# The skip term D u written into the sum's PSUM bank by ScalarE, TensorE's state sums added onto it

## The reference, cut to what matters

```python
delta = softplus(dt @ W_dt.T + b_dt)          # 1024 inner channels, 128 positions
def step(h, ins):                             # 16 states for each inner channel
    d_t, B_t, C_t, u_t = ins
    dA = exp(d_t[..., None] * A)
    h = dA * h + (d_t * u_t)[..., None] * B_t[:, None, :]
    y_t = einsum('bds,bs->bd', h, C_t)        # sum over the 16 states
    return (h, y_t)
y = scan(step) + u * Dp                       # the skip term D u
y = y * silu(z)                               # the gate
return y @ W_out.T
```

## Time and profile before

| | |
|---|---|
| median of 3 runs | 4119.69 us (4118.02 to 4127.19) |
| the profiled execution | 4124.45 us |
| its span, first to last instruction | 4122.3 us |
| mean granted TensorE clock | 0.95 of full speed |
| busy: TensorE, VectorE, ScalarE, GpSimd | 87%, 88%, 70%, 84% of the span |

### The profile page before, as it was taken

One profiled execution on the slowest core, in us unless ns is written; L12 is line 12 of the kernel. 1 busy time (PEld: TensorE's weight loads), 2 busy tenths in 40 slices (PEclk: granted clock), 3 DMA queues, 4 the chain that ended last, 5 costly groups with the idle time before them and its releaser, 6 DMA issues. The chain is left out here.

```text
span 4122.3 us, 44370 instructions
## 1 busy us (share of the span) xinstructions
PE 3597.6 (87%) x11386; PEld 2046.1 (50%) x11386; DVE 3607.9 (88%) x3165; ACT 2868.8 (70%) x6098; POOL 3455.2 (84%) x1860
## 2 busy tenths in 40 slices
PE   6888888988888988888988888988888988888887
PEld 3644554545554545554544554554554554554443
DVE  0499988999989999889998989999999899989898
ACT  1577667777667777667777667777767777767775
POOL 0298888898888998888998888898888898888899
PEclk8899999999999999999999999999999999999999
DMA  2111101111101111101111101111101111101110
GB/s 100 49 51 53 53 9 47 50 53 53 53 8 48 50 53 53 53 8 48 50 53 53 53 8 48 50 53 53 53 9 47 50 53 53 53 8 44 47 47 8
DMA packets 50702, 183.68 MB, mean 45 GB/s; under 512 B 7339, under 2 KB 33203, under 8 KB 42067
## 3 DMA queue, kind: packets, MB, share of 16 engines
q1 hardware_dynamic: 48880, 174.17, 11.0%
q10 hardware_dynamic: 1636, 7.83, 0.5%
HBM read 164.15 MB, written 17.83 MB: 44 GB/s over the span
## 5 line engine op out<-in xcount | busy, mean ns | idle before, releaser
L411 POOL TENSOR_TENSOR st<-st,bc 128x1024 f32<-128x1024 f32 x1024 | 2399.4, 2358 | 474.2 <-DVE st L870 473.0
L870 DVE TENSOR_TENSOR_SCAN st<-dec,st 128x1024 f32<-128x1024 f32 x1024 | 2311.9, 2277 | 78.0 <-ACT dec L464 63.6
L464 ACT ACTIVATE dec<-delta,decay 128x254 f32<-128x254 f32 x4096 | 1695.1, 465 | 713.4 <-DVE st L870 712.4
L685 PE MATMUL y_ps<-st,ident 128*128 128x512 f32 x4096 | 1975.9, 611 | 184.2 <-POOL st L411 182.8
L685 PEld LDWEIGHTS y_ps<-st,ident 128*128 128x128 f32 x4096 | 756.5, 194 | 999.8 <-issue 599.7
L858 DVE TENSOR_TENSOR st<-du,bc 128x1024 f32<-128x1024 f32 x736 | 885.5, 1203 | 34.3 <-ACT du L450 34.3
L402 POOL TENSOR_TENSOR st<-du_sb,bc 128x1024 f32<-128x1024 f32 x288 | 679.3, 2359 | 0.1
L896 DVE SCALAR_TENSOR_TENSOR u<-d_ps,chan,u 128x250 f32<-128x250 f32 (+2 forms) x768 | 309.4, 473 | 160.9 <-ACT u L504 159.2
L705 PE MATMUL g<-wo,zs 128*128 128x256 f32 x1024 | 300.2, 446 | 0.8 <-DVE zs L877 0.8
L705 PEld LDWEIGHTS g<-wo,zs 128*128 128x128 f32 x1024 | 230.8, 229 | 128.8 <-issue 92.1
L681 PE MATMUL y_ps<-u,diag 128*128 128x256 f32 x512 | 168.5, 459 | 127.7 <-DVE zs L877 127.6
(11 more groups left out here) (106 smaller groups left out, 2775.1 us busy)
## 6 DMA issues: line engine op xcount, KB each, us to landing
bc<-bc_dram SPq DMA_DIRECT2D x64, 2048.0 KB, 9.8
xg<-x_dram SPq DMA_DIRECT2D x32, 256.0 KB, 11.5
x_dram<-xg SPq DMA_DIRECT2D x32, 256.0 KB, 2.0
last_x<-x_dram SPq DMA_DIRECT2D x32, 256.0 KB, 2.6
out_dram<-last_x SPq DMA_DIRECT2D x32, 256.0 KB, 2.1
bc<-w_inT_dram ACTq DMA_DIRECT2D x1, 4096.0 KB
adjt<-adjT_dram SPq DMA_DIRECT2D x32, 128.0 KB, 11.2
bc<-w_out_dram ACTq DMA_DIRECT2D x1, 2048.0 KB
```

Source lines behind the costliest of these rows:

```text
L411: nc.gpsimd.tensor_tensor(st[:, sl, :, :, :], st[:, sl, :, :, :], bc[:, p, 1, SU * q:SU * q + SU, None, :].to_broadcast([P, SU, 2, T]), AL ...
L464: a = nc.scalar.activation(dec[:, v % 2, s, j, :].rearrange("p (b t) -> p b t", b=PAIR)[:, :, 1:], delta[:, p, 2 * i + j, :].rearrange("p ...
L685: mm = nc.tensor.matmul(y_all, ident[:, :], st[:, sl, s, :, :].rearrange("p j t -> p (j t)"), start=False, stop=(q == Q - 1 and s == SU - ...
L870: nc.vector.tensor_tensor_scan(h, dec[:, v % 2, :, :, :].rearrange("p s j t -> p (s j t)"), h, 0.0, ALU.mult, ALU.add).then_inc(S["scanned ...
```

## The change

ScalarE writes D u of the block into `y_ps` with two Copy activations that take D as a scale for each partition, in step 8i + 2 after the decays of unit 8i + 3 and ahead of the dense work of that step. It waits for the gate of the block before; TensorE's first state sum of a block waits for ScalarE's write instead of that gate. All state sums add. One matmul ahead of the first group writes the whole bank, so that its columns count as written. The diagonal weights, which VectorE made at the start, are gone.

```diff
+PRIME_STEP = 25
+SKIP_STEP = 2
...
-        diag = sb("diag", [P, J, P])
...
+            def skip_term(act, k, p, i):
+                if i == 0:
+                    wait(act, "silu_u", k + 1)
+                    if isinstance(k, int) and k == 0:
+                        act.wait_ge(S["y_primed"], 1)
+                wait(act, "y_gated", JP * k + i)
+                for j in range(2):
+                    a = nc.scalar.activation(y_ps[:, j, :], u[:, p, 2 * i + j, :], ACT.Copy,
+                                             scale=chan[:, TAPS + 2, 2 * i + j:2 * i + j + 1])
+                a.then_inc(S["skipped"], 1)
...
                     if scan and v + 1 < U:
                         decays(act, k, p, v + 1)
+                    if scan and v % Q == SKIP_STEP:
+                        skip_term(act, k, p, v // Q)
                     if dense:
                         dense_act(act, k + 1, r, v)
...
+            def prime(pe):
+                wait(pe, "wo_folded", JP)
+                nc.tensor.matmul(y_all, ident[:, :], wxz[:, 0, 0:512], start=True, stop=True).then_inc(S["y_primed"], 1)
...
                         fold_wo(pe, v)
+                        if v == PRIME_STEP:
+                            prime(pe)
...
                 if q == 0:
-                    wait(pe, "y_gated", JP * k + i)
-                    if isinstance(k, int) and k == 0 and i == 0:
-                        pe.wait_ge(S["diag_made"], J)
-                        pe.wait_ge(S["wo_folded"], JP)
-                    for j in range(2):
-                        nc.tensor.matmul(y_ps[:, j, :], diag[:, 2 * i + j, :], u[:, p, 2 * i + j, :],
-                                         start=(j == 0), stop=False, skip_group_check=True)
+                    wait(pe, "skipped", JP * k + i + 1)
...
-                    for j in range(J):
-                        nc.vector.tensor_scalar(diag[:, j, :], ident[:, :], chan[:, TAPS + 2, j:j + 1], None, ALU.mult)\
-                            .then_inc(S["diag_made"], 1)
```

More of the change, by code:

```diff
@@ L178, in build @@
         names = """stands w_graph w_dense memsets reps_made attn_mm attn_made fold_mm folded bias_mm bias_row bias_stored bias_loaded wo_mm wo_folded bconv_made edged edge_part decay_exp decay_neg
-        dec_zeroed diag_made x_loaded adj_loaded stats aggr veps_made rstd_pow rstd_made normed transposed xT_made xnT_made
+        dec_zeroed y_primed skipped x_loaded adj_loaded stats aggr veps_made rstd_pow rstd_made normed transposed xT_made xnT_made
         e_mm e_exp alpha_max alpha_made rowsum_mm u1_mm rowsum_eps rinv_made x1k_made u1T_mm u1T_made u2T_mm u2T_made
```

## The result

The changed kernel takes 4270.88 us (median of 4 runs, 4266.37 to 4274.76) where the kernel before takes 4120.6 us beside it: a ratio of 1.0362, 95% interval 1.0344 to 1.0380, so 150 us slower. The forecast was slower, at 4230 us in a range of 4145 to 4270; the time lies 1 us above its upper end. The profiled execution takes 4274.76 us, its span is 4272.6 us and its mean granted clock 0.926 in place of 0.950.

What follows compares the result with a forecast made beforehand. No single engine bounds the kernel: TensorE and GpSimd lead from step 26 to the group's end, VectorE elsewhere. Step 26's 2.95 us plus step 10's 0.6, times 31 groups, add 110 us: 4230 us, range 4145 to 4270.

Steps and rivals of the forecast that it cites:

- none at 18: Gate of step 18: no loss, as ScalarE's skip term is done at 2110.9, the old one on TensorE at 2111.02.
- The skip term behind ScalarE's eight decays: Gate of step 26: Copies queue behind the decays of units 26 and 27, so the first state sum starts 2.56 us later.
- ScalarE's reads of z waiting: Behind the gate of step 26: ScalarE's reads of z wait for TensorE by microseconds in place of 0.39 us.
- the scan of unit 12 waiting: After the gate of step 10: silu(u) and its table loads push the decays, so VectorE's scan is 1.04 us late.
- the pair of Copies: ScalarE's write of the skip term at each gate: between 0.81 and 0.93 us, taken as 0.9.
- the rival in which the clock holds: Step 26: TensorE keeps its clock, only 2.56 us late; with step 10, 30 to 62 us, 4149 to 4182; chance 0.20.
- slower still: Half speed lasts 5.1 us or more, step 10's loss stays whole, step 2's slow stretch is longer: 158 us, 4278; chance 0.07.
- step 10's loss: Gate of step 10: scan of unit 12 1.04 us late, partly taken back by step 26; 0.6 us a group taken.
- The clock's term at step 26: TensorE idles 4.9 us, then runs at half speed: 1.5 to 2.6 us of work lost a group, 2.0 taken.
- The stretch from the gate of step 2 on: Gate of step 2: counted 0, bounds 0 and 0.9 us gained, as the slow time falls on the state sums instead.
- the absorption: Part of step 10's 1.04 us is taken back at step 26, where VectorE idles 1.50 us for ScalarE; 0.6 us left.
- no change: Losses at steps 26 and 10 are absorbed by unseen idle times or paid by step 2: within 8 us; chance 0.05.

Runs made afterwards that it cites:

- three runs of blocks on TensorE: Changed kernel with the skip term of block 3, block 1, or blocks 1 and 3 back on TensorE: 1.0216, 1.0329 and 1.0071 of the kernel before.
- kernels kept warm: Extra overwritten matmuls while TensorE would idle: kernel before in steps 1, 8 (0.9736); blocks 1, 3 on TensorE, same (0.9758); changed kernel, also step 25 (0.9874).
- Holding the clock there alone: Changed kernel with four extra matmuls, result overwritten, on TensorE in step 25 while it waits for step 26's skip term: 1.0204 of the kernel before.
- the other order: Changed kernel with ScalarE's skip term behind silu(u) in step 10 and ahead of the decays of unit 27 in step 26: 1.0234 of the kernel before.

## Why the prediction was right, and where it was short

*Direction, places and waits: right.* All three runs of blocks on TensorE put the loss where it was forecast: at the gates of steps 26 and 10, none at 18. The skip term behind ScalarE's eight decays (2.43 us late, 2.56 forecast), ScalarE's reads of z waiting up to 5.20 us, the scan of unit 12 waiting 1.08 us (1.04), the pair of Copies in 0.85 to 0.88 us (0.9): each as worked out. In the kernels kept warm the change costs 48 to 57 us, where the rival in which the clock holds had 30 to 62. In the changed kernel itself, where step 10 costs more (below), the gates put the part that is not the clock at 0.95 + 1.30 = 2.25 us a group, 70 us.

*The size: 110 us forecast, 150 measured.* The time lies at the rival "slower still" (4278, chance 0.07) and not near the forecast of 4230; the range held it but for 1 us because it took in a part of that rival. Its three terms are those that turn out short: half speed of more than 5.1 us at step 26 (in half of the groups), step 10's loss in full, and 0.5 us for a longer slow stretch in 2 to 10. By the table of gates 5.13 - 3.55 = 1.58 us a group are missing. Three terms were short, and two of them are the clock.

The clock's term at step 26 was 2.0 us a group. Holding the clock there alone gave back 2.25 us in 26 to 2, and 65 to 75 us in all. The term was 0.25 us short in 26 to 2, where TensorE lost a mean of 2.33 us of work; nearly all of it was felt.

The stretch from the gate of step 2 on was put at nothing, as the slow time would only fall on other matmuls. It costs 0.63 us in 2 to 10, and with blocks 0 and 2 alone on ScalarE 0.87. Kept warm, the same two blocks cost 0.17 there (37.07 against 36.90). So the Copies themselves are nearly free there, as forecast, and the slow stretches, which I took to keep their length, did not. Most of the loss is not at the gate of step 2, which alone the prediction priced: 0.11 us is the taps' wait there, 0.53 the wait of the gate of step 10 behind the slow stretch of step 8. As the mean clock shows it, the work that TensorE can have lost to half speed (idle time at the low clock is counted in) is at most (1 - 0.950) x 4122.3 = 206 us before, 316 us after and 240 us with blocks 1 and 3 on TensorE.

Step 10's loss was taken at 0.6 us a group, as partly absorbed by the 1.50 us that VectorE idled for ScalarE at step 26. It is not absorbed: ScalarE is pushed as well. VectorE's idle time there grew from a mean of 1.41 us to 1.83; with block 1 back on TensorE it is 1.40. With the clock held at step 26, 33.02 - 31.51 = 1.51 us stay in 26 to 2, 0.56 more than the 0.95 of the wait there; with 0.74 in 10 to 18 step 10 costs some 1.3 us, 0.7 more than was taken and more than the upper bound of 1.04. The 0.56 is a difference, not measured by itself; the 0.62 that block 1 back on TensorE took from 26 to 2 agrees with it. This is the step of the forecast that failed: the absorption. The prediction says that ScalarE is pushed too, but still took 0.44 us off.

Two slips lie in the prediction's reading. It took one group for all, but 2 to 10 differs already before, from 40.8 to 43.2 us, and the taps' wait of 2.86 us has a mean of 3.29. And its range leaves out 0.13 below and not 0.08, as "no change" lies below 4145 too.

The Trainium skill (TensorE: Matmul & The Clock Gate, "What's actually happening") puts the cost of the clock's ramp at under 1% of a typical kernel span. This kernel is not such a case, as half speed comes back in every group: the 65 us given back at one place are 1.5% of the span, the 108 us at the two places of the kernel before 2.6%.

*What stays open:* why the slow stretch of step 8 is longer in half of the groups of the changed kernel. Its idle time is the same 5.36 us. The one at step 2 is longer (a mean of 4.58 us in place of 2.72, of which 1.04 is that the sum now waits for the Copies), but no run here holds the clock in one of the two places alone.

## What to carry to other kernels

An instruction moved to an engine with time to spare is worth what that engine's queue is doing at the moment when its input is ready: here 0.9 us of work behind 3.25 us of decays, on the busiest stretch of the engine that it was to relieve. Where a new wait lets TensorE idle for some microseconds, price the half speed that follows, in that place and in the places whose timing shifts. Where TensorE waits in every round of a loop, a few matmuls into a free bank can be worth more than any work taken off it: they made the kernel before 2.6% faster.

## What the runs showed of the hardware

The same idle time costs the clock in one place and not in another: 2.02 us kept it in the kernel before, 2.03 us lost it in seven of 28 groups of the run with block 3 on TensorE; 3.06 us lost it in the run with the other order. Half speed behind a restart lasted from 2.9 us to 7.6 us, and after the same idle time of 5.36 us it lasted 5.1 us in a group of the kernel before and 7.6 in one of the changed kernel. A Copy with a scale for each partition from SBUF into PSUM, 128x256, takes 0.47 us, and 0.85 to 0.88 us as a pair.
